# Queries, keys and values of three attentions: high and low parts in two 128-row tiles, values between the units, four banks each, three products per position row

## The reference

```
x = x + conv_attention(ln(x), L0)          # "c0": attention with relative positions
x = x + experts(ln(x), L0)                 # "f0": 8 experts, top 2
x = x + conv_attention(ln(x), L1)          # "c1"
h = ln(x) * g + b;  x = x + attention(h)   # "f1": attention without positions
x = x + mlp(x);  x = x + experts(ln(x))    # "mlp", "moe"

def conv_attention(x, ...):                # b = 4, 12 heads of 16, 1024 tokens
    q, k, v = split_heads(x @ qkv_w.T + qkv_b)
    rel_h = einsum('bnhwc,hkc->bnhwk', q, Rh)     # 32 rows of a table for each row
    rel_w = einsum('bnhwc,wkc->bnhwk', q, Rw)     # ... and for each column
    attn  = softmax(q k.T * 16**-0.5 + rel_h[..., :, None] + rel_w[..., None, :])
    return (attn v) @ proj_w.T + proj_b
```

## Time and profile before

| | us |
|---|---|
| median of 3 runs | 3806.86 (3805.78 to 3816.05) |
| the profiled execution | 3804.64 |
| its span, first to last instruction | 3803.1 |
| PE busy | 3146.3 (83%) |
| DVE busy | 2664.5 (70%) |
| ACT busy | 2032.5 (53%) |
| mean granted TensorE clock | 0.902 of full speed |

### The profile page before, as it was taken

How to read it: one execution, slowest core, us unless ns; L and a number is a source line. 1 busy time by engine, 2 the same in 40 slices (tenths; PEclk the granted TensorE clock), 3 DMA queues, 4 the chain that set the end, 5 groups by cost and what they waited for, 6 DMA issues and landing times. The chain is left out here.

```text
span 3803.1 us, 66407 instructions
## 1 busy us (share of the span) xinstructions
PE 3146.3 (83%) x20240; PEld 1407.1 (37%) x20240; DVE 2664.5 (70%) x5142; ACT 2032.5 (53%) x2719; POOL 278.2 (7%) x363
## 2 busy tenths in 40 slices
PE   4748999986999999464899998346999996869998
PEld 2422222233666666341222223221222224636666
DVE  5458899966666666445889896638999974556555
ACT  3516677764433333341667676343777773455554
POOL 0010111110000000001011111001111110000000
PEclk9759999997999999675999999576999998979999
DMA  2274667742000000037476764010111111020000
GB/s 59 99 173 83 139 133 144 142 92 72 21 0 0 0 0 0 25 102 173 82 139 131 140 141 98 8 67 27 48 51 44 53 40 28 1 63 9 4 8 13
DMA packets 179968, 251.98 MB, mean 66 GB/s; under 512 B 50974, under 2 KB 73646, under 8 KB 179850
## 3 DMA queue, kind: packets, MB, share of 16 engines
q1 hardware_dynamic: 155642, 213.65, 25.4%
q0 software_dynamic: 13104, 17.60, 2.3%
q10 hardware_dynamic: 11104, 19.28, 1.4%
HBM read 182.80 MB, written 66.65 MB: 66 GB/s over the span
## 5 line engine op out<-in xcount | busy, mean ns | idle before, releaser
L734 DVE TENSOR_REDUCE c1att_mx<-c1att_m 128x1 f32<-128x512 f32 x768 | 493.9, 685 | 64.9 <-PE c1att_m L672 59.7
L734 DVE TENSOR_REDUCE c0att_mx<-c0att_m 128x1 f32<-128x512 f32 x768 | 493.4, 685 | 61.9 <-PE c0att_m L672 56.8
L734 DVE TENSOR_REDUCE f1att_mx<-f1att_m 128x1 f32<-128x512 f32 x768 | 493.3, 685 | 26.5 <-PE f1att_m L672 21.8
L973 ACT ACTIVATE c1att_p<-c1att_s 128x1024 f32<-128x1024 f32 x384 | 372.1, 1021 | 155.7 <-PE c1att_s L687 155.6
L973 ACT ACTIVATE c0att_p<-c0att_s 128x1024 f32<-128x1024 f32 x384 | 372.1, 1021 | 151.9 <-PE c0att_s L687 151.7
L973 ACT ACTIVATE f1att_p<-f1att_s 128x1024 f32<-128x1024 f32 x384 | 372.1, 1021 | 119.6 <-PE f1att_s L687 118.6
L1392 ACT ACTIVATE f_s<-f_u 128x512 f32<-128x512 f32 x192 | 114.6, 597 | 373.5 <-PE f_u L1317 373.5
L1481 DVE SCALAR_TENSOR_TENSOR f_h<-f_u,f_s 128x512 f32<-128x512 f32 x192 | 132.6, 691 | 149.5 <-ACT f_s L1392 145.6
L1400 ACT ACTIVATE moe_h<-moe_u,moe_bu 128x512 f32<-128x512 f32 x192 | 136.5, 711 | 175.8 <-PE moe_u L1317 93.8
L700 PE MATMUL c1att_o<-c1att_p,c1att_vs 128*32 128x512 f32 x1536 | 208.5, 615 | 0.6 <-ACT c1att_p L973 0.6
L700 PE MATMUL c0att_o<-c0att_p,c0att_vs 128*32 128x512 f32 x1536 | 207.5, 613 | 0.6 <-ACT c0att_p L973 0.6
(11 more groups left out here) (488 smaller groups left out, 5963.4 us busy)
## 6 DMA issues: line engine op xcount, KB each, us to landing
xt<-rel_parts SPq DMA_DIRECT2D x256, 128.0 KB, 7.4
xt<-qk_parts SPq DMA_DIRECT2D x192, 128.0 KB, 5.0
y<-rel_parts SPq DMA_DIRECT2D x128, 128.0 KB, 5.4
y<-qk_parts SPq DMA_DIRECT2D x96, 128.0 KB, 4.8
c0att_qm<-rel_parts SPq DMA_DIRECT2D x144, 64.0 KB, 2.2
c1att_qm<-rel_parts SPq DMA_DIRECT2D x144, 64.0 KB, 2.2
rel_parts<-c0qkv_rhi SPq DMA_DIRECT2D x48, 128.0 KB, 2.3
rel_parts<-c0qkv_rlo SPq DMA_DIRECT2D x48, 128.0 KB, 2.3
```

What stands on the lines that cost most here:

```text
L734: dve.tensor_reduce(mx[:, n:n + 1], bank[:, :], AX.X, ALU.max).then_inc(s_mx, 1)
L973: act.activation(pr[h][kt % 2][:, :], sps[h][:, :], ACT.Exp).then_inc(s_e, 1)
```

## The change

- The tiles `queries` and `keys` become `high` and `low`, both of 128 rows: query rows 0 to 63 and key rows 64 to 127 in each. ScalarE writes `high` with one instruction of 128 rows in place of two of 64, VectorE writes `low` with one in place of two.
- TensorE's and VectorE's lists interleave: a unit, then a tile of values, three times, then the fourth tile of values.
- The banks `qp` and `vp` become four each; the two added to each are the banks `rp` of the position rows. The position rows therefore wait for the last value (`s_vt`) as well.
- As `queries` no longer holds both parts on one set of 128 rows, a position row takes three products: `th` x `high`, `tl` x `high`, `th` x `low`. The lower halves of all four tables are zero, written by GpSimd at the stage's start; ScalarE writes two tables instead of four halves.
- `rhi` and `rlo` get a second buffer for the middle group, in room that the caller lends (the two tiles `xt`).
- The scratch of the position rows has the direction k outermost instead of second. Stores and loads of it have the same shapes.

```diff
-        queries, keys = m.sb("q", GROUPS * T, F16), m.sb("k", GROUPS * T, F16)
-        qp = [m.ps(f"qp{u}") for u in range(2)]
-        vp = [m.ps(f"vp{u}") for u in range(2)]
+        high, low = m.sb("high", GROUPS * T, F16), m.sb("low", GROUPS * T, F16)
         rp = [m.ps(f"rp{u}") for u in range(4)]
+        qp = [m.ps(f"qp{u}") for u in range(2)] + rp[0:2]
+        vp = [m.ps(f"vp{u}") for u in range(2)] + rp[2:4]
...
-                        for s, part, buf, at_row in ((0, 0, queries, 0), (0, 1, queries, GW),
-                                                     (1, 0, keys, GW), (1, 1, keys, 0)):
-                            sp.dma_start(scratch["qk"][s, row:row + GH, part, :, :],
...
+                        for s, at_row in ((0, 0), (1, GW)):
+                            for part, buf in enumerate((high, low)):
+                                sp.dma_start(scratch["qk"][s, row:row + GH, part, :, :],
...
-                                        rows = scratch["rel"][g * GH + b * NH:(g + 1) * GH + b * NH, k, half, part]
+                                        rows = scratch["rel"][k, b * NH + g * GH:b * NH + (g + 1) * GH, half, part]
...
+                    for g in range(GROUPS):
+                        turned(c, g)
+                        values(4 * c + g)
+                    values(4 * c + GROUPS)
                 if not rel:
                     return
-                pe.wait_ge(s_tabs, 4)
-                pe.wait_ge(s_wh, 6)
-                pe.wait_ge(s_lo, 2 * CHUNKS * GROUPS)
+                pe.wait_ge(s_tabs, 2)
+                pe.wait_ge(s_zero, 5)
+                pe.wait_ge(s_vt, TILES)
+                pe.wait_ge(s_lo, CHUNKS * GROUPS)
...
-                                pe.matmul(out, th[k][:, reach], row_of(q, k, r), start=True, stop=False)
-                                ins = pe.matmul(out, tl[k][:, reach], row_of(q, k, r), start=False, stop=True)
+                                pe.matmul(out, wh, row_of(top, k, r), start=True, stop=False)
+                                pe.matmul(out, wl, row_of(top, k, r), start=False, stop=False)
+                                ins = pe.matmul(out, wh, row_of(rest, k, r), start=False, stop=True)
...
-                        dve.tensor_tensor(queries[GW:P, cols], qt[n % 3][0:GW, :], queries[0:GW, cols],
-                                          ALU.subtract).then_inc(s_lo, 1)
-                        dve.tensor_tensor(keys[0:GW, cols], qt[n % 3][GW:P, :], keys[GW:P, cols],
-                                          ALU.subtract).then_inc(s_lo, 1)
...
+                        dve.tensor_tensor(low[:, cols], qt[n % 3][:, :], high[:, cols], ALU.subtract).then_inc(s_lo, 1)
...
-                        for buf, rows in ((queries, slice(0, GW)), (keys, slice(GW, P))):
-                            act.activation(buf[rows, at(c, g)], qp[n % 2][rows, :], ACT.Identity,
-                                           bias=bias[rows, g:g + 1], scale=gain[rows, 0:1]).then_inc(s_hi, 1)
+                        act.activation(high[:, at(c, g)], qp[n % 4][:, :], ACT.Identity, bias=bias[:, g:g + 1],
+                                       scale=gain[:, 0:1]).then_inc(s_hi, 1)
...
-                        if g:
-                            act.wait_ge(s_rst[k], g * 256)
+                        if g == 2:
+                            act.wait_ge(s_rst[k][0], 256)
```

More of the change, by code:

```diff
@@ L249, in _, with qkv @@
                         ins.then_inc(s_turned, 1)
-def qkv(nc, name, parts, vt, w, scratch):
+def qkv(nc, name, parts, vt, w, scratch, spare=None):
     rel = "rel_h" in w
@@ L277, in qkv @@
         s_rel, s_rhi, s_rlo = m.sem("rel"), m.sem("rhi"), m.sem("rlo")
-        s_rst = [m.sem(f"rst{u}") for u in range(2)]
+        s_rst = [[m.sem(f"rst{k}{u}") for u in range(2)] for k in range(2)]
         if rel:
@@ L285, in qkv @@
             own = m.sb("own", GH, parts=GW)
-            rhi = [m.sb(f"rhi{k}", T, F16) for k in range(2)]
-            rlo = [m.sb(f"rlo{k}", T, F16) for k in range(2)]
+            rhi, rlo = ([[m.sb(f"{n}{k}", T, F16)[:, :], t[:, k * T:(k + 1) * T]] for k in range(2)]
+                        for n, t in zip(("rhi", "rlo"), spare))
         vt4 = vt[:, :].rearrange("p (a k f) -> p a k f", a=PAIRS, k=KT)
@@ L341, in _ @@
                 pool.memset(scale[GW:P, :], 1.0).then_inc(s_init, 1)
+                pool.wait_ge(s_init, 2)
+                for i, t in enumerate(th + tl if rel else ()):
+                    pool.memset(t[GW:P, :], 0.0).then_inc(s_zero, 1)
+                    pool.wait_ge(s_zero, i + 2)
             @block.tensor
@@ new lines, in values @@
+                def values(t):
+                    if t >= 4:
+                        pe.wait_ge(s_vt, t - 3)
+                    bank, tokens = vp[t % 4][:, 0:C], slice(t * P, (t + 1) * P)
+                    pe.matmul(bank, xa_hi[:, tokens], ah[:, 2 * C:W], start=True, stop=False)
+                    pe.matmul(bank, xa_hi[:, tokens], al[:, 2 * C:W], start=False, stop=False)
+                    pe.matmul(bank, xa_lo[:, tokens], ah[:, 2 * C:W], start=False, stop=False)
+                    pe.matmul(bank, xb[:, tokens], bh[:, 2 * C:W], start=False, stop=False)
+                    pe.matmul(bank, xb[:, tokens], bl[:, 2 * C:W], start=False, stop=True).then_inc(s_v, 1)
@@ L463, in _ @@
                         for k in range(2):
-                            for rows in (slice(0, GW), slice(GW, P)):
-                                act.activation(th[k][rows, :], tab[k][:, :], ACT.Identity).then_inc(s_wh, 1)
+                            act.activation(th[k][0:GW, :], tab[k][:, :], ACT.Identity).then_inc(s_wh, 1)
                 if not rel:
@@ L612, in load_maxima @@
                     row = base + (2 + half) * HD
[L613 removed]
+                    src = scratch["rel"][1, head, half, 0].rearrange("a r n -> (a r) n").unsqueeze(1)
                     sp.dma_start(qm[u][row:row + QSIDE, :].rearrange("p (v n) -> p v n", v=halves),
@@ L1616, in conv @@
             stages.append(lambda: layer_norm(nc, l + "ln", x, 1e-6, stats, xt, idn, parts=thirds(y), direct=True))
-            stages.append(lambda: qkv(nc, l + "qkv", thirds(y), vt, w, scratch))
+            stages.append(lambda: qkv(nc, l + "qkv", thirds(y), vt, w, scratch, hidden))
             stages.append(lambda: attention(nc, l + "att", vt, True, scratch, a["hot"], ident16[:, :], by_pool, x, a[f"{l}_wo"],
```

77 lines of the change are left out of this document (37 added, 40 removed).

## The result

The changed kernel takes 3700.0 us, median of 4 runs (3690.95 to 3707.48); the kernel before, run beside it, 3807.5 (3805.8 to 3816.1). The ratio is 0.9712 with a 95% interval of 0.9686 to 0.9739: 2.9% faster, with 3698 predicted.

A forecast was written before the change was run, and what follows sets the result against it. It saw engines taking turns in the unit loop, strided reads pacing k = 1 position rows, and stores binding f1. c0 and c1 -75.4 and f1 -34 give -109 from 3804.64: 3695.6, median 3698; range 3683 to 3712, with neighbours 3665 to 3740.

The forecast's parts named there:

- The unit loop: c0's unit loop: TensorE without gaps, 4.9 us a chunk at full clock, 40.3 us in place of 100.5.
- The rival of a clock that isn't held: Unit loop at 1.2 GHz: 9.7 us a chunk, loop 78, total 3786; chance 5%.
- The new wait: Before the position rows: the first product waits for the last values, some 2.3 us, new.
- The position rows: c0's three groups of each k with 96 products: 85.8 us against 65.8 before, 20.0 more.
- the second k = 0 group: Position rows, behind a k = 1 group: first 20 products step at 0.104 us, the rest at half, 6.1 us.
- SyncE's backlog: c0's stores of units last until 130, six position groups until 191; products' way ends at 193.2, stores 2 us short of binding.
- The stores in f1: f1's stores bind: 66 us of data at 95 GB/s, 2 to land, ending at 2531 for 2565.3: -34 us.
- The rival of starving attention: Attention's loads of position rows slow down with the scratch's new pitch between heads (128 KB for 256): total 3900; chance 2%.
- The sum: All three stages: -75.4 us in c0 and c1 together, -34 in f1, -109 in all; median 3698.

The follow-up runs named there:

- two-product kernel: The changed kernel without the third product of the position rows (term table x low part left out of the computation): 3688.5 us, ratio 0.9680.
- the reshaped stores: The changed kernel with the part as outer dimension of the queries and keys scratch, a store being 64 rows in place of 4 x 16: 3668.0 us, ratio 0.9628.
- the old order: The changed kernel with the scratch of position rows in the old order, direction k second again: 3697.3 us, ratio 0.9713.
- tiles only: The changed kernel with the old order of lists and two banks each; 128-row tiles, three products and second buffers stay: 3741.0 us, ratio 0.9827.
- the kernel with contiguous operands: The changed kernel with the k = 1 position rows' moving operand read from 128 neighbouring tokens, not every 16th: 3684.8 us, ratio 0.9688.

## Why the prediction was right

- *The unit loop, 42.6 us to the first position row.* Measured 42.7 and 43.5. Steps of 1.49 for a unit with a tile of values and 1.90 with two make 4.9 a chunk, with the clock at 1.00. The 128-row copy in float16, for which the trace before had no row, takes 0.77 us, and a unit of ScalarE 1.49 in the pace of TensorE, 1.32 when it catches up (0.66 + 0.66); I had taken 1.47 of 1.27 to 1.47. The rival of a clock that isn't held is refuted. What I had not seen is what made up before's loop: I put it down to the turns alone, and 1.8 us of a chunk were the clock behind each pause.
- *The new wait, +2.3.* It is 1.9 (the wait at 97.23).
- *The position rows, 85.8.* From 97.23 to SyncE's start on the last 16 stores at 184.83 are 87.6. The k = 1 groups are right to the tenth (102.58 to 124.88: 22.3). The mis-sized term is the second k = 0 group: I gave 20 products to the lower clock, and 42 had it (124.88 to 129.34), 7.5 us for 6.1; the third took 6.3. Before, too, this number wasn't steady: 20 behind the first strided group, the row that I took, and 35 behind the second.
- *SyncE's backlog.* Predicted to last until 130 and to be 2 us short of binding; it lasted until 123.85 and was 6.4 us short. The two-product kernel shows the limit behind it: 139.4.
- *The stores in f1.* 66 us at 95 GB/s and 2 to land were predicted; from the first issue at 2388.70 to the landing at 2454.7 they took 66.0, and f1 gained 35.7 for 34. That it fits so closely is in part luck: with a backlog the rate is 102 GB/s (2396 to 2440), and SyncE first waits 4.5 us, in four pieces, for later units. The quarter of the engines, which I took from the share of 0.26 and the rule beside it, is shown by the reshaped stores: the trace agrees with the Trainium skill, "DMA: Bandwidth & Descriptors", section "Why a DMA increments its semaphore by 16 and not by 1".
- *The scratch's pitch.* The rival of starving attention had 2%; the old order gives the same stages.
- *The sum.* -72.3 in c0 and c1 for -75.4, -35.7 in f1 for -34: two small errors of opposite sign. That the median came within 2 us of 3698 is luck as well, as single runs lie between 3691 and 3707.

The parts do not add up, which the prediction didn't say. The order and banks alone bring 94.7 us of stage time, the tiles with three products and the second buffers 68.6, all together 108.0. They shorten the same loop (c0's first position row comes after 63.0 and 61.6 us, with all after 42.7, before after 100.5), and behind it stand the stores, whose bytes neither changes.

## What to carry to other kernels

When two engines take turns at a pair of banks, either more banks or an interleaved order can end it, as each did here; try one and see who is late next, as a queue of transfers that hid in the pauses may set the end. Where the clock falls in a pause of TensorE, price the pause with the slower work behind it (1.8 us a chunk here), not only with its length. And look at the share of the transfer engines of a store whose outer dimension is small: one index moved in the scratch was worth 27 us in f1, three quarters of what the whole change brought there.

## What the runs showed that I had not expected

- TensorE kept its full clock through a pause of 1.71 us in each chunk and worked at the lower level behind pauses of 4.34 us (tiles only, before). Between the two lies no sharp rule: behind the pause of 1.9 us at the loop's end the changed kernel stayed at the full clock, the kernel with contiguous operands was at the lower one from 98.6 to 102.0. In the position rows it came back from the lower level after 4.5 us of dense work in one group (124.88 to 129.34) and 2.0 us in the next (154.66 to 156.66), in the same program.
- With a backlog, SyncE issues a 128 KB store on the quarter of the engines every 1.28 us on average (eight from 108.19 to 118.47) instead of every 0.64: the queue slows to the pace of the data (131 KB at 102 GB/s), and everything behind it in SyncE's list waits too. GpSimd's issue of such a store takes 0.51.
- ScalarE copies 128 x 512 into float16 in 0.77 us modelled at steps of 0.66 to 0.80, and 64 x 512 in the same 0.76 to 0.77: the number of rows doesn't show in the time, so one instruction in place of two halves it.
